# A gated delta rule layer on one core: nV, the product of v and the root of its gate term, is made on GpSimd instead of VectorE, with new orders of steps on all engines

## What is computed

```python
qkvz = (xn @ w_qkvz.T)            # 32 heads, q, k, v, z of 64 each
q, k, v = causal_conv4(q, k, v)   # 4 taps for each channel, along the sequence
q = l2norm(q) * 64 ** -0.5
k = l2norm(k)
g = -exp(A_log) * softplus(a + dt_bias); beta = sigmoid(b)
for t in range(256):              # for each batch and head
    S = S * exp(g[t])
    delta = (v[t] - k[t] @ S) * beta[t]
    S = S + outer(k[t], delta)
    o[t] = q[t] @ S
o = o * rsqrt(mean(o * o) + EPS) * norm_weight * sigmoid(z)
out = x + o @ w_out.T + ffn(xn)   # ffn: Hadamard transforms, silu(gate) * up, down
```

## Time and profile before

| | |
|---|---|
| median of three runs | 813.8 us (813.3 to 815.29) |
| the profiled execution | 817.35 us, of it 815.2 us from the first to the last instruction |
| mean granted clock of TensorE | 0.983 |
| busy: TensorE, its weight loads, VectorE, ScalarE, GpSimd | 742.0, 485.2, 694.7, 326.5, 278.8 us |

### The profile page before, as it was taken

The page is one execution under the profiler, slowest core; times in us unless marked ns, Lnnn a source line. Parts: engine busy times, 40 slices in busy tenths (PEclk is TensorE's granted clock), DMA queues, the critical chain, the costliest instruction groups (busy, mean ns, idle before and its releaser), DMA issues.

```text
span 815.2 us, 26961 instructions
## 1 busy us (share of the span) xinstructions
PE 742.0 (91%) x11562; PEld 485.2 (60%) x11562; DVE 694.7 (85%) x1224; ACT 326.5 (40%) x737; POOL 278.8 (34%) x185
## 2 busy tenths in 40 slices
PE   1779989989899999999999999999999998989986
PEld 1535555756566565656566576666566565657664
DVE  4789998999899988998989988998988888887645
ACT  2235434444344345352534444353534362444120
POOL 3015411525252434325161424234252516234110
PEclk9979999999999999999999999999999999999979
DMA  7123050414242231404131231404123232312201
GB/s 223 58 65 88 24 99 24 91 37 71 64 85 50 36 99 27 101 10 84 56 80 42 46 95 22 106 15 82 40 38 98 29 105 29 73 21 31 42 2 53
DMA packets 140406, 49.79 MB, mean 61 GB/s; under 512 B 118144, under 2 KB 131840, under 8 KB 140160
## 3 DMA queue, kind: packets, MB, share of 16 engines
q1 hardware_dynamic: 139664, 47.93, 26.1%
q10 hardware_dynamic: 624, 0.15, 0.1%
HBM read 40.44 MB, written 7.60 MB: 59 GB/s over the span
## 4 chain that ended last, share of the span: by engine, by line
PE 54%; DVE 30%; issue 7%; ACT 4%; POOL 3%; DMA 1%; SPq 1%; DVEq 0%; ACTq 0%; POOLq 0%
PE bank L716 17%; DVE kq L259 11%; PE bank L737 4%; PE bank L807 4%; PE bank L916 4%; PE bank L836 3%; PE bank L803 3%; PE bank L864 3%; PE bank L805 3%; PE bank L744 2%; PE bank L767 2%; PE bank L849 2%; PE bank L819 1%; PE bank L943 1%; PE bank L780 1%
## 5 line engine op out<-in xcount | busy, mean ns | idle before, releaser
L716 PE MATMUL bank<-xnT,wq 128*128 128x512 f32 x512 | 254.3, 622 | 6.6 <-DVE kq L259 6.3
L259 DVE SCALAR_TENSOR_TENSOR kq<-bank,cw,kq 128x510 f32<-128x510 f32 (+2 forms) x288 | 213.6, 745 | 14.6 <-ACT kq L1044 7.7
L716 PEld LDWEIGHTS bank<-xnT,wq 128*128 128x128 f32 x512 | 89.8, 192 | 88.0 <-issue 71.2
L1044 ACT ACTIVATE kq<-bank,cw 128x512 f32<-128x512 f32 x96 | 65.9, 686 | 135.4 <-PE bank L716 132.3
L1232 POOL TENSOR_TENSOR Sd<-St,dec 128x256 f32<-128x256 f32 x32 | 20.8, 649 | 268.4 <-DVE St L383 218.7
L1226 POOL TENSOR_TENSOR kqg<-kq,rows 128x1024 f32<-128x1024 f32 x32 | 77.1, 2423 | 77.2 <-DVE kq L259 42.1
L1236 POOL TENSOR_TENSOR ost<-ost,cst 128x8 f32<-128x8 f32 x32 | 55.0, 1718 | 92.1 <-DVE ost L396 91.4
L916 PE MATMUL bank<-wo,oT 128*128 128x256 f32 x256 | 68.4, 384 | 0.1
L737 PE MATMUL bank<-xh,wguT 128*128 128x512 f32 x128 | 59.4, 607 | 1.6 <-DVE hf L271 1.6
L371 DVE TENSOR_TENSOR X<-UT,bank 128x256 f32<-128x256 f32 (+1 forms) x96 | 43.4, 461 | 17.5 <-PE bank L807 9.6
L916 PEld LDWEIGHTS bank<-wo,oT 128*128 128x128 f32 x256 | 45.9, 190 | 17.2 <-issue 12.1
(11 more groups left out here) (129 smaller groups left out, 1254.5 us busy)
## 6 DMA issues: line engine op xcount, KB each, us to landing
wq<-wqkvz_dram SPq DMA_DIRECT2D x16, 512.0 KB, 3.9
rows<-decay_rows SPq DMA_DIRECT2D x64, 128.0 KB, 3.0
rows<-decay_rows SPq DMA_DIRECT2D x32, 256.0 KB, 4.2
inverse_blocks<-UU SPq DMA_DIRECT2D x32, 128.0 KB
UT<-inverse_blocks SPq DMA_DIRECT2D x128, 32.0 KB, 2.4
wguT<-wgu_dram SPq DMA_DIRECT2D x8, 256.0 KB, 3.6
woraw<-wout_dram SPq DMA_DIRECT2D x16, 128.0 KB, 2.5
base_blocks<-ATP SPq DMA_DIRECT2D x128, 16.0 KB, 1.8
```

Of the source, the lines that this page charges most:

```text
L259: nc.vector.scalar_tensor_tensor(out=y[:, :, t:S], in0=p[:, :, 0:S - t], scalar=cw[:, m, i // 2, 3 - t:4 - t], in1=y[:, :, t:S], op0=ALU.m ...
L716: last = nc.tensor.matmul(ring[i % 2][:], wq[:, q, kc, i // 2, :], xnT[:, kc, (i % 2) * 512:(i % 2) * 512 + 512], start=kc == 0, stop=kc = ...
L1044: nc.scalar.activation(kq[:, i // 2, 2 * (i % 2):2 * (i % 2) + 2, :], split(ring[i % 2][:], 2), ACT.Copy, scale=cw[:, m, i // 2, 3:4]).the ...
```

## The change

The step vtr leaves VectorE's list and enters GpSimd's with the same waits and the same product. The engine that makes nV is thereby another; vt, the root and nV keep their tiles, with as many buffers as before. The orders of all five lists are written anew; no other step is added, dropped or altered. The core of the diff, with the orders cut to one period of the middle (pairs 6 to 8):

```diff
-                def vtr(m, q, H):
-
-                    dve.wait_ge(vt_done, m * 8 + 4 * H + 4)
-                    dve.wait_ge(root_done, m + 1)
-                    wait(dve, dl_ready, (m - 2) * 4 + 1)
-                    wait(dve, y_done, (m - 1) * 3)
-                    nc.vector.tensor_tensor(nV[:, q, half(H)], vt[:, half(H)], over(stat[:, 2, half(H)]), ALU.mult).then_inc(nv_done, 1)
...
+                def vtr(m, q, H):
+
+                    wait(pool, dl_ready, (m - 2) * 4 + 1)
+                    wait(pool, y_done, (m - 1) * 3)
+                    pool.wait_ge(root_done, m + 1)
+                    pool.wait_ge(vt_done, m * 8 + 4 * H + 4)
+                    nc.gpsimd.tensor_tensor(nV[:, q, half(H)], vt[:, half(H)], over(stat[:, 2, half(H)]), ALU.mult).then_inc(nv_done, 1)
```

More of the change, by code:

```diff
@@ L980, in _ @@
[L980 to L982 removed]
+                         "state": state, "o": o, "turn": turn, "out": out, "wd": wd, "fo": fo}, """0.decays 0.proj.0 0.proj.1 0.wd.0 0.proj.2 0.ktr.0 0.wd.1 0.proj.3 0.ff 0.proj.4 0.ktr.1 0.proj.5 1.ff 0.proj.6
@@ new lines, in _ @@
+                     0.delta.2 2.proj.5 0.state.2 2.proj.6 0.ks.3 0.delta.3 0.turn.0 2.gram.0 0.o.1.0 0.o.1.1 0.o.1.2 0.out.0 2.proj.7
+                     2.gram.1 0.turn.1 0.out.1 2.vtr.0 0.out.2 0.out.3 3.proj.0 3.proj.1 1.hz.0.0 1.hz.0.1 1.hz.1.0 1.hz.1.1 2.qsq 1.hz.2.0
+                     1.hz.2.1 3.proj.2 1.hz.3.0 1.hz.3.1 3.proj.3 1.delta.0 2.vtr.1 1.state.0 3.proj.4 1.ks.1 1.delta.1 3.ktr.0 1.state.1
+                     1.o.0.0 1.o.0.1 3.ktr.1 1.ks.2 1.o.0.2 3.proj.5 1.delta.2 1.state.2 3.proj.6 1.ks.3 3.gram.0 1.delta.3 1.turn.0
@@ L1025, in _ @@
[L1025 to L1028 removed]
+                     7.proj.2 5.ks.1 6.qsq 5.delta.1 7.ktr.0 5.state.1 5.o.0.0 5.o.0.1 5.ks.2 5.o.0.2 7.proj.3 5.delta.2 6.vtr.1 5.state.2
@@ new lines, in _ @@
+                     7.proj.4 5.ks.3 7.ktr.1 7.proj.5 5.delta.3 5.turn.0 5.o.1.0 5.o.1.1 5.o.1.2 7.proj.6 7.gram.0 5.out.0 7.proj.7
+                     5.turn.1 5.out.1 5.out.2 7.ff 5.out.3 6.hz.0.0 6.hz.0.1 7.gram.1 6.hz.1.0 6.hz.1.1 6.hz.2.0 6.hz.2.1 6.hz.3.0 8.proj.0
+                     6.hz.3.1 8.proj.1 6.delta.0 7.vtr.0 6.state.0 8.proj.2 6.ks.1 7.qsq 6.delta.1 7.vtr.1 6.state.1 6.o.0.0 6.o.0.1 6.ks.2
+                     6.o.0.2 8.proj.3 6.delta.2 8.proj.4 6.state.2 8.ktr.0 6.ks.3 8.proj.5 6.delta.3 8.ktr.1 6.o.1.0 6.o.1.1 6.turn.0
@@ new lines, in _ @@
+                     6.o.1.2 8.proj.6 6.out.0 8.gram.0 8.proj.7 6.turn.1 6.out.1 6.out.2 8.ff 6.out.3 7.hz.0.0 7.hz.0.1 8.gram.1 7.hz.1.0
+                     7.hz.1.1 7.hz.2.0 7.hz.2.1 7.hz.3.0 9.proj.0 7.hz.3.1 9.proj.1 7.delta.0 8.vtr.0 7.state.0 9.proj.2 7.ks.1 8.qsq
+                     7.delta.1 8.vtr.1 7.state.1 7.o.0.0 7.o.0.1 7.ks.2 7.o.0.2 9.proj.3 7.delta.2 9.ktr.0 7.state.2 9.proj.4 7.ks.3
+                     7.turn.0 9.ktr.1 7.delta.3 9.proj.5 7.o.1.0 7.o.1.1 7.o.1.2 9.proj.6 7.out.0 9.gram.0 9.proj.7 7.turn.1 7.out.1
@@ new lines, in _ @@
+                     7.out.2 9.ff 7.out.3 8.hz.0.0 8.hz.0.1 9.gram.1 8.hz.1.0 8.hz.1.1 8.hz.2.0 8.hz.2.1 8.hz.3.0 10.proj.0 8.hz.3.1
+                     10.proj.1 8.delta.0 9.vtr.0 8.state.0 10.proj.2 8.ks.1 9.qsq 8.delta.1 9.vtr.1 8.state.1 8.o.0.0 8.o.0.1 8.ks.2
+                     8.o.0.2 10.proj.3 8.delta.2 10.ktr.0 8.state.2 10.proj.4 8.ks.3 10.ktr.1 8.delta.3 10.proj.5 8.turn.0 8.o.1.0 8.o.1.1
+                     8.o.1.2 10.gram.0 10.proj.6 8.out.0 10.proj.7 8.turn.1 8.out.1 8.out.2 10.ff 8.out.3 9.hz.0.0 9.hz.0.1 10.gram.1
@@ new lines, in _ @@
+                     9.hz.1.0 9.hz.1.1 9.hz.2.0 9.hz.2.1 9.hz.3.0 11.proj.0 9.hz.3.1 11.proj.1 9.delta.0 10.vtr.0 9.state.0 11.proj.2
+                     9.ks.1 10.qsq 9.delta.1 10.vtr.1 9.state.1 9.o.0.0 9.o.0.1 9.ks.2 9.o.0.2 11.proj.3 9.delta.2 11.ktr.0 9.state.2
+                     11.proj.4 9.ks.3 11.ktr.1 9.delta.3 9.turn.0 11.proj.5 9.o.1.0 9.o.1.1 9.o.1.2 11.proj.6 11.gram.0 9.out.0 11.proj.7
+                     9.turn.1 9.out.1 9.out.2 11.ff 9.out.3 11.gram.1 10.hz.0.0 10.hz.0.1 11.vtr.0 12.proj.0 12.proj.1 10.hz.1.0 10.hz.1.1
@@ new lines, in _ @@
+                     11.hz.3.1 12.qsq 11.delta.0 11.state.0 13.proj.2 11.ks.1 12.vtr.1 13.proj.3 11.delta.1 13.ktr.0 11.state.1 11.o.0.0
+                     11.o.0.1 11.o.0.2 13.proj.4 11.ks.2 13.proj.5 11.delta.2 13.ktr.1 11.state.2 13.proj.6 11.ks.3 11.delta.3 11.turn.0
+                     11.o.1.0 11.o.1.1 11.o.1.2 13.gram.0 11.out.0 13.proj.7 13.gram.1 11.turn.1 11.out.1 13.vtr.0 11.out.2 11.out.3
+                     14.proj.0 14.proj.1 12.hz.0.0 12.hz.0.1 14.proj.2 12.hz.1.0 12.hz.1.1 13.qsq 12.hz.2.0 12.hz.2.1 12.hz.3.0 12.hz.3.1
```

293 lines of the change are left out of this document (133 added, 160 removed).

## The result

The changed kernel takes 841.6 us (median of four runs, 839.0 to 847.6) where the kernel before takes 814.5 beside it: a ratio of 1.034, 95% interval 1.028 to 1.040. The forecast was 818.2, with a range up to 824. The direction was right, the size was not: 27 us in place of 4.4.

What follows compares the result with a forecast made beforehand. TensorE was taken to bound the kernel, 97% busy in the middle, with VectorE mattering only where TensorE waits. 6.4 - 2.5 + 0.5 + 0 = +4.4 us on the 813.8 median gave 818.2, range 806 to 824.

Steps and rivals of the forecast that it cites:

- the meetings: nV's first half on GpSimd blocks VectorE's inv, delaying Y and delta.1: eight times 0.8 us, +6.4, bounds 0 to 10.
- the orders: Moved steps in the engines' lists, some hundreds: net 0 us, bounds -6 to +5.
- count for pair 6: Pair 6 has two blockers, nV and kd.1 behind sd.1, so it counts twice among the eight.
- The relief of VectorE: nV leaves VectorE, 32 instructions and 34.6 us busy; shorter TensorE waits gain 2.5 us, bounds 0 to 10.
- those named as won: TensorE waits directly behind nV: yacc L439 0.68 us, ATP L309 0.6, yacc L421 0.7.
- Nothing late behind the second half of nV: On GpSimd ahead of kd and root, the second half is covered: nV done about 423.5 us, first used 435.5.
- The norm behind nV: Late pairs: nV's second half precedes the previous pair's norm, which VectorE's gated step awaits: +0.5 us, bounds 0 to 3.
- (3): Rival: late pairs' meetings and the norm behind nV are exposed too, +3 and +2 us, 823 us; chance 0.04.
- The sign named for being wrong: Forecast wrong if L342 stays at 0.17 us or TensorE's idle time from 245 to 606 us falls below 10.

Runs made afterwards that it cites:

- e1: The changed kernel with nV's first half behind sd.2 on GpSimd in every pair, and kd.1 of pair 6 ahead of sd.1: 828.5 us, ratio 1.017.
- e2: The kernel before with its old orders and only nV moved to GpSimd, at places clear of inv: 818.0 us, ratio 1.004.
- e4: e2 with nV's first half directly behind sd.1, the place of the change: 826.6 us, ratio 1.016.
- e15: The kernel before plus one unneeded 128x512 GpSimd product directly behind sd.1 of pairs 3 to 9: 828.1 us, ratio 1.017.
- e9: e1 with 128 more waits, met at once, ahead of all of TensorE's work: 820.2 us, ratio 1.005.
- e12: The changed kernel with 128 more waits, met at once, ahead of all of TensorE's work: 833.3 us, ratio 1.023.
- e5: The changed kernel with unneeded 2-column matmuls in TensorE's wait ahead of delta.1, pairs 4 and 6 to 10: 837.3 us, ratio 1.027.
- e10: The changed kernel with unneeded 128x512 matmuls in TensorE's wait ahead of delta.1, pairs 4 and 6 to 10: 836.6 us, ratio 1.027.
- e11: The kernel before with 128 more waits, met at once, ahead of all of TensorE's work: 818.3 us, ratio 1.005.

## Why the prediction was wrong

What made up the 27 us, by medians: net 814.8 - 802.5 = 12.3, of which 5.7 are the meetings (after to e1), 7.4 the orders (e1 to e2), -0.8 the move itself (e2 to before); lost to the clock 26.9 - 11.4 = 15.5, of which 7.5, 2.2 and 5.8 at the same three steps. The parts of the clock are rough, since the loss varies by some 11 us between runs of one kernel.

- **The meetings** (forecast +6.4): right in mechanism, places, count for pair 6, and size (5.7 net; 5.0 in e4; 4.8 for seven in e15). Their whole price was 9 to 15 us (8.6 in e4, 13.1 in e1, 15.0 in e15), since the clock also falls behind some of them. The bound of 10 us for them was too low for that reason alone.
- **The relief of VectorE** (forecast -2.5): mis-sized, none is measured (0.8 us net, inside the spread). VectorE's busy time fell as said (677.2, a little above the 660 to 670 named), but the waits for taps stayed (5.2 us), and of those named as won the one for ATP grew, from 0.6 us to 4.9 (L770).
- **Nothing late behind the second half of nV**: right. GpSimd's 32 products take 1.04 us each, and root waits no more. The norm behind nV (+0.5) makes VectorE wait longer, 6.0 us in five waits where the earlier trace rows has 3.0 in four, and TensorE's own wait for og is 1.2 us, so little of it seems to have got through (no run has this step alone):

```profile
DVE og L394 <- POOL ost L1233: 6.0, 5, 1.8
```

- **The orders** (forecast 0, bounds -6 to +5): wrong, 7.4 net. Some hundreds of moves were put down at nothing because the trace of before doesn't show their waits. About half goes with the places of the unnamed waits among small matmuls (3.8 of 7.4 in e9), which the lists don't show; beside them the waits for d grew (6.7 us in place of 4.3) and one for turn came (1.4). How much of the rest each of these carries was not measured.
- **The clock** is the step that failed first: it had no term, and the runs show 15.5 us of the 27 in it. The sum took a pause of 0.8 us to cost 0.8 us. The earlier trace rows showed 1.00 in the middle, and I took that for a constant of the kernel, not for something that the new waits could change. The mean clock of 0.983 in the table ahead of the prediction could have told that the kernel before already loses 14 us to it.
- **The rivals**: (3), more than forecast, was nearest in kind, and its 823 was still 18 us short. The sign named for being wrong didn't show: TensorE's idle time from 250 to 620 us is 19.8 us, not below 10. Both the prices of a wait and the bounds of the orders came from terms taken one by one, without the clock that all of them share.

## What to carry to other kernels

Where TensorE is at 97%, a new pause among small matmuls can cost more than its own length, since half speed sometimes follows: in these runs pauses of 0.8 to 1.0 us came to 1.5 to 2 times that. So put a term for the clock into the sum and compare kernels with and without their loss to it. A GpSimd product with a read of 1.04 us behind one of 0.64 held up a VectorE instruction of 8 elements on the way to Y: put such a product where VectorE's next result has slack (e2 against e4: 8.6 us by one place in the list). A rewritten order isn't free because its work is the same; test it apart from the move that it was made for.

## What the runs showed of the hardware

- The clock fell behind pauses of 0.78 us (412.7 us in the kernel after) and 1.01 us (e15), and in e5 at two places where 2-column matmuls had left no pause (458.2 and 509.4 us); at the six places of e10 with 128x512 ones it didn't. It doesn't fall behind each pause: with the same lists it fell in pairs 2, 6, 7 and 10 in the kernel after and in pairs 6, 7, 8 and 9 in e12. The Trainium skill (TensorE: Matmul & The Clock Gate, A second HAM failure mode: psum-queue depth-cycling) tells of a kernel whose short idle times between groups of matmuls make the clock go down and up. The rows with a pause agree; the two places of e5 without one are nothing that it tells of.
- The spread of one kernel's runs is mostly that loss: e2 811.5 to 822.1 us, 799.2 to 803.8 net.
- 128 instructions that do nothing, ahead of all of TensorE's work, changed the time by -8 us (e9, e12) and +4 us (e11: 818.3 beside 814.4), in e11 all of it in the clock (15.5 lost in place of 12.2, net the same).
- Open: why the same pause is followed by half speed in one pair and not in the next; why e2 and e11 lost more than the kernel before; and that the refills cause the unnamed waits is inferred, not shown.
